# S4D convolution on one Trainium2 core: the load of x moved from the first to the last place in the sync engine's slot

## What is computed

```python
mask = (arange(L) < length[:, None])
u = x * mask[:, None, :]
K = 2 * einsum('hn,hnl->hl', Cs, exp(dtA[:, :, None] * arange(L))).real   # one kernel of length L per channel
y = irfft(rfft(u, 2L) * rfft(K, 2L))[..., :L] + u * D[:, None]            # causal convolution per channel
out = x + y * mask[:, None, :]
```

## Time and profile before

| What | Value |
|---|---|
| Time, median of 3 runs | 970.13 us (968.56 to 974.08) |
| The profiled execution's own time | 973.51 us |
| Its span in the trace | 971.7 us |
| Mean granted TensorE clock | 0.982 of full speed |
| Busy share PE / PEld / DVE / ACT / POOL | 86% / 82% / 78% / 69% / 62% |
| DMA queue of SP (q1) | 152.15 MB, 64.2% of 16 engines |
| Instructions | 22927 |

### The profile page before, as it was taken

How to read it: one execution, slowest core, us unless ns; L and a number is a source line. 1 busy time by engine, 2 the same in 40 slices (tenths; PEclk the granted TensorE clock), 3 DMA queues, 4 the chain that set the end, 5 groups by cost and what they waited for, 6 DMA issues and landing times.

```text
span 971.7 us, 22927 instructions
## 1 busy us (share of the span) xinstructions
PE 836.0 (86%) x6281; PEld 794.9 (82%) x6281; DVE 759.9 (78%) x2041; ACT 669.3 (69%) x1720; POOL 605.3 (62%) x843
## 2 busy tenths in 40 slices
PE   0679988898888988898988989889898898988897
PEld 0579987898888888888887888888788888888896
DVE  8757877778778787777877878787787878787887
ACT  4567766667677676766767667676667777776774
POOL 5746755656666666665666656666566666666663
PEclk9779999999999999999999999999999999999999
DMA  4126866666667676766766667676666767676674
GB/s 95 43 60 155 171 153 172 163 150 172 165 158 180 152 182 156 173 167 155 178 153 168 171 158 178 153 181 156 165 174 160 178 158 182 157 181 152 167 184 111
DMA packets 161393, 152.71 MB, mean 157 GB/s; under 512 B 13656, under 2 KB 161240, under 8 KB 161240
## 3 DMA queue, kind: packets, MB, share of 16 engines
q1 hardware_dynamic: 161064, 152.15, 64.2%
q10 hardware_dynamic: 304, 0.26, 0.1%
HBM read 84.02 MB, written 67.30 MB: 156 GB/s over the span
## 4 chain that ended last, share of the span: by engine, by line
DMA 54%; SPq 29%; issue 7%; DVE 4%; PE 3%; ACT 2%; POOL 0%; DVEq 0%; ACTq 0%; POOLq 0%
DMA out_dram<-xall 53%; SPq L361 18%; SPq L366 10%; DMA traw<-krows 1%; SPq L378 1%; PE v L1209 1%; SPq L422 0%; ACT room L588 0%; PE y L1093 0%; PE v L1093 0%; ACT zhi L727 0%; DVE zlo L1008 0%; ACT B L588 0%; PE y L1095 0%; PE y L1094 0%
## 5 line engine op out<-in xcount | busy, mean ns | idle before, releaser
L588 ACT ACTIVATE room<-v 64x192 f32<-64x192 f32 (+1 forms) x768 | 235.7, 307 | 155.5 <-PE v L1095 74.9
L1093 PE MATMUL y<-fhi,zhi 128*128 128x256 f32 x511 | 164.8, 323 | 92.2 <-DVE zlo L1008 91.7
L963 DVE SCALAR_TENSOR_TENSOR mid<-room,RV,v 128x192 f32<-128x192 f32 (+2 forms) x512 | 183.4, 358 | 68.7 <-ACT room L588 61.6
L963 DVE SCALAR_TENSOR_TENSOR v<-v,RV,mid 128x192 f32<-128x192 f32 (+2 forms) x512 | 191.1, 373 | 38.6
L952 DVE COPY_PREDICATED xall<-mask,y 128x512 f32<-128x512 int32 x254 | 190.4, 750 | 2.4 <-issue 2.4
L1093 PEld LDWEIGHTS y<-fhi,zhi 128*128 128x128 f32 x511 | 97.6, 191 | 112.1 <-issue 112.1
L1093 PE MATMUL y<-thi,uhi 128*128 128x256 f32 x511 | 176.1, 345 | 0.0
L1008 DVE SCALAR_TENSOR_TENSOR zlo<-v,RV,zhi 128x448 fp32r<-128x448 f32 x128 | 87.5, 684 | 82.3 <-ACT zhi L727 81.4
L1095 PE MATMUL y<-fhi,zlo 128*128 128x256 f32 x511 | 145.4, 284 | 0.0
L1094 PE MATMUL y<-flo,zhi 128*128 128x256 f32 x511 | 144.9, 284 | 0.0
L1095 PE MATMUL y<-thi,ulo 128*128 128x256 f32 x511 | 144.1, 282 | 0.0
(11 more groups left out here) (217 smaller groups left out, 2167.4 us busy)
## 6 DMA issues: line engine op xcount, KB each, us to landing
xall<-in_x_dram SPq DMA_DIRECT2D x256, 256.0 KB, 4.3
out_dram<-xall SPq DMA_DIRECT2D x254, 256.0 KB, 4.2
traw<-krows SPq DMA_DIRECT2D x128, 128.0 KB, 4.5
NXY<-B SPq DMA_DIRECT2D x2, 512.0 KB, 6.2
krows<-ksb SPq DMA_DIRECT2D x8, 1.0 KB, 2.5
krows<-ksb SPq DMA_DIRECT2D x8, 4.0 KB, 3.6
krows<-ksb SPq DMA_DIRECT2D x8, 11.0 KB, 3.7
out_dram<-xall SPq DMA_DIRECT2D x1, 128.0 KB, 2.5
```

The source lines that it names most:

```text
L588: return act.activation(dst, src, ACT.Copy)
L963: return dve.scalar_tensor_tensor(out=out, in0=src, scalar=RV[:, k:k + 1, h], in1=other, op0=ALU.mult, op1=ALU.add)
L1093: pe.matmul(o, a_hi, b_hi, start=start, stop=False, skip_group_check=True)
```

## The change

In SP's slot of channel h the step that loads x of channel h+4 stands last, behind the store of channel h-1 and the load of T of channel h+2. Its condition, its wait and its two DMAs are the same. Nothing else is touched.

```diff
             def slot(g, j):
                 h = chan(g, j)
                 early = isinstance(g, int) and g < 2
-                if exists(g, j, 4) and not (early and h + 4 < SLOTS):
-                    sp.wait_ge(s_out[(j + 4) % SLOTS], 32 * on(g, j, 4)[0])
-                    load_x(*on(g, j, 4))
                 if early and 2 <= h <= 5:
                     sp.wait_ge(s_kfin, 2)
...
                 if exists(g, j, -1):
                     sp.wait_ge(s_pred, 2 * h)
                     store(*on(g, j, -1))
                 if exists(g, j, 2):
                     sp.wait_ge(s_intra, h + 1)
                     load_t(*on(g, j, 2))
+                if exists(g, j, 4) and not (early and h + 4 < SLOTS):
+                    sp.wait_ge(s_out[(j + 4) % SLOTS], 32 * on(g, j, 4)[0])
+                    load_x(*on(g, j, 4))
```

## The result

The changed kernel takes 888.23 us (887.13 to 889.85), the kernel before 970.85 us in the same comparison: a ratio of 0.915, 95% interval 0.912 to 0.918. The forecast was 885 us with 876 to 908; the time moved as forecast.

The account below looks back on a forecast made before the run. SP's turn of two issues and a store's landing, 6.93 us, was taken as the bound; 970.1 - 87.0 = 883.1, with some 2 us for late landings of T, gave 885 us, range 876 to 908.

Parts of the forecast that it names:

- The turn of SP: On SP, one loop of issuing x, issuing the store and its landing, 6.93 us, claimed to bound the kernel.
- The wait moved last: On SP, x's wait for a store issued some 9 us before, landing in 3.2 to 5.1; claimed to cost nothing.
- The ring of the engines: The compute engines' cycle between TensorE's products from the state, via ScalarE's thi and zhi, then zlo: 6.37 us in the loop.
- the sum: Over 120 slots, 108 at 6.37 and 12 at 6.28 make 763.3 us in place of 850.3: 87.0 less.
- T lands in 3.4: SP's load of T in its new place: landing in 3.4 us with about 4.4 available, costing nothing.
- the nearest row: Profile row taken for T's landing: the early one, median 3.4 us, as the store is issued well over 2 us before.
- The thin cover of x: SP's load of x before TensorE's even transposes: slack 0.1 to 1.5 us, where it had been over 5; no cost.
- The clock breaks: Drops of the granted clock after TensorE idles in long waits for T; three, 4.7 us together, claimed to go.
- TensorE's wait for zlo: TensorE's wait before products from the state, claimed to fall from 91.7 us to some 20 to 35.
- Rival 1: On the DMA queue, T stays last, landing in 5.1 to 5.6 us; time 921 to 951 us; chance 0.14.

## Why the prediction was right, point by point

*The turn of SP is the bound.* Right, and shown from both sides: the turn made shorter by one issue gives 893 us with the wait kept; the path from T to zhi cut gives 972.

*The wait moved last costs nothing.* Right: it does not appear among SP's waits.

*The ring of the engines is what is left, 6.37 in the loop and 6.28 outside.* Right to 0.02: the median of the loop is 6.39. The 120 slots were to take 763.3 us and took 767.0. Of the 3.7 some 2.4 are these 0.02 in 107 slots; 1.2 are two late loads of x. The saving is 83.2 in the slots and 82.6 between the medians, where the sum had 87.0. The 2 us that the forecast added for late landings of T stood for something that did not happen; that they brought it nearer to 888 is luck. One figure of the range is off: by its own sum 878 to 898 us is a slot of 6.32 to 6.49, not 6.33 to 6.47. The profiled pair differs by 86.4, for the prologue was 3.2 us shorter in that execution (thi of channel 7 at 105.43 in place of 108.58); other executions here have it at 106.7 to 112.3.

*T lands in 3.4 and costs nothing.* Right: 3.6 in the middle, 4.0 at most there and 4.5 in the whole run, no wait. The choice of the nearest row, T issued when the issue of the store in front had ended some 2 us before, was the step on which this rested; with x in between, the same DMA was late in 86 channels. One reading beside it was wrong: the 5.1 of the earlier trace rows were put beside the small kernel stores, but in that trace these go out from 56.8 to 130.8 us, so they are in the stretch with 3.4 too, and from 160 to 200 us, without them, T still took a median of 5.0. In the changed kernel T landed in 3.2 to 3.6 from 113 to 131 us, where four of them went out.

*The thin cover of x.* Right in kind. Expected was a landing of 4.3; it rose to 4.6 to 4.8. Its second DMA started 1.05 to 1.76 us behind the product from the state, where 1.3 to 1.8 were expected. No transpose was to wait, and two did, 0.52 us at 108.70 and 0.38 at 140.72, in slots 0.7 and 0.5 us too long. The loads of x that they waited for took up to 6.7 and 6.5 us to land. Why was not found; only the first was issued beside small kernel stores:

```profile
108.70 0.66 PE L1078 MATMUL xt_even<-ident,xall 128*128 128x128 f32 x4 [0.52 <-DMA xall<-in_x_dram]
```

*The clock breaks go.* Right: the granted clock averages 1.00 from 200 to 800 us, and no slot of the loop is 1.5 us too long.

*TensorE's wait for zlo would stay at 20 to 35 us.* Wrong: the list has 1.2 us. A break is still there, but shorter than the 0.15 to 0.25 us expected: 0.10 us (the last Toeplitz pair ends at 401.97, the next product starts at 402.07), and PE is idle for 9.9 us in 94 slots. The list puts it down to no wait of PE; at the same product it has an idle time of the weight loads, put down to "issue" (32.5 us of PEld, 123 times).

*Rival 1, a fuller queue.* The load did rise to 185 GB/s and a share of 0.78, and T landed sooner. Where T landed later, it was with more standing directly in front of it and a lower mean load (4.6 us at 174 GB/s in the order store, x, T). The step that the Trainium skill names for high load (DMA: Bandwidth & Descriptors, Latency and other measured facts) is not seen at this rate: stores landed in a median of 3.3 us, against 4.2 before, though their place in the queue changed as well, and no run tells whether this rate is what the page calls high.

## What to carry to other kernels

When a queue's program has a wait for its own earlier transfer, write down its turn: landing plus every issue between. If that is longer than the engines' turn it is the bound, and one issue less in it can be nearly as good as the wait removed (893 us against 888). Of the steps behind it, put the one with the nearest deadline first and the one that nobody waits for last (with the store ahead of x it was 952 us), and test a cover by its longest landings, not by the median; and after such a gain look at the order on the compute engines again, since an exchange worth nothing before (972 us) was worth 11 us after (888 to 878).

## What the runs showed that I had not expected

The 128 KB load of T landed in 3.6 us behind a store 2 us old, 4.2 with 256 KB of x put between, and 4.6 with 512 KB, while the mean load fell, from 185 over 179 to 174 GB/s. With T first, issued 2.3 us or more behind the last issue of x, it was 2.9 us (median, at 170 GB/s). And with half of x in front it had a tail up to 7.1 us that the other two orders, at 4.0 and 5.6, did not have. That tail was not explained.
